# Interleaving the per-head Q/K projections with the attention loop of the head before

## The reference

```python
c_q  = x @ W_DQ                                  # latent 256
Qc   = (c_q @ W_UQ)  -> 16 heads of 64
Qr   = rope(c_q @ W_QR) -> 16 heads of 32
c_kv = x @ W_DKV
Kc   = (c_kv @ W_UK) -> 16 heads of 64
Kr   = rope(x @ W_KR)                            # 32, shared by all heads
V    = (c_kv @ W_UV) -> 16 heads of 64
Q, K = concat([Qc, Qr]), concat([Kc, Kr])        # 96 wide
scores  = clip(Q K^T, -80, 80), causal mask
weights = softmax(scores / sqrt(96))
x = layernorm(x + (weights V) @ W_O)
x = layernorm(x + ffn(x))     # two 8-bit fake-quantised LoRA layers, exact gelu
```

## Time and profile before

| | us |
|---|---|
| median of 3 runs (2410.88 to 2481.31) | 2411.21 |
| the profiled execution | 2413.98 |
| its span on the slowest core (6) | 2412.4 |
| spans of the 8 cores | 2397.9 to 2412.4 |

### The profile page before, as it was taken

How to read it: one execution, slowest core, us unless ns; L and a number is a source line. 1 busy time by engine, 2 the same in 40 slices (tenths; PEclk the granted TensorE clock), 3 DMA queues, 4 the chain that set the end, 5 groups by cost and what they waited for, 6 DMA issues and landing times.

```text
span 2412.4 us, 28275 instructions; the slowest of 8 cores (2397.9 to 2412.4 us)
## 1 busy us (share of the span) xinstructions
PE 1425.3 (59%) x7027; PEld 703.0 (29%) x7038; DVE 1061.8 (44%) x1381; ACT 844.8 (35%) x1165; POOL 83.5 (3%) x136
## 2 busy tenths in 40 slices
PE   0073566666666666564444224331698888988986
PEld 0020122122221222121111002111465655655754
DVE  2257565566665566676445573444212012012012
ACT  0000254444454344450335305555233233233241
POOL 0000000000000000000000000000000000000000
PEclk9576677666677666675665555555798998988987
DMA  5500011111111111412222002323000000000000
GB/s 174 144 6 0 13 51 42 44 55 43 54 43 43 39 60 38 133 38 90 82 75 63 22 10 70 88 87 88 14 19 19 1 19 18 1 19 18 1 18 18
DMA packets 49661, 112.28 MB, mean 47 GB/s; under 512 B 12528, under 2 KB 23280, under 8 KB 47200
## 3 DMA queue, kind: packets, MB, share of 16 engines
q0 software_dynamic: 14912, 54.53, 7.3%
q1 hardware_dynamic: 24800, 34.96, 5.0%
q10 hardware_dynamic: 9792, 20.98, 2.9%
HBM read 97.47 MB, written 8.39 MB: 44 GB/s over the span
## 4 chain that ended last, share of the span: by engine, by line
PE 40%; DVE 24%; ACT 15%; DMA 11%; issue 8%; DVEq 1%; ACTq 1%; SPq 0%; POOLq 0%
PE PSD L314 28%; DVE CL L657 6%; PE PS L314 4%; ACT PT L663 4%; PE BIG L571 4%; DMA QSG<-wPRr 4%; ACT QSG L760 3%; DVE MXW L529 3%; PE PSD L641 3%; DMA QSG<-wFCr 3%; DVE KH L498 2%; DVE CL L650 2%; ACT QH L487 2%; ACT QTI L764 1%; DMA STG<-xT 1%
## 5 line engine op out<-in xcount | busy, mean ns | idle before, releaser
L663 ACT ACTIVATE PT<-CL 128x1024 bf16<-128x1024 f16 (+1 forms) x320 | 310.7, 971 | 363.1 <-DVE CL L650 217.9
L314 PE MATMUL PSD<-XT,RTF 128*128 128x256 bf16 x2048 | 307.9, 300 | 121.7 <-ACT HH L1086 119.8
L641 PE MATMUL PSD<-QH,KH 96*128 96x512 bf16 (+3 forms) x640 | 241.7, 476 | 95.6 <-DVE CL L650 86.9
L571 PE MATMUL BIG<-PT,VP 128*65 128x512 bf16 (+3 forms) x640 | 221.9, 437 | 104.0 <-ACT PT L663 101.6
L314 PE MATMUL PSD<-HH,RTP 128*128 128x256 bf16 x2048 | 237.3, 275 | 53.8 <-DVE UPt L1103 53.8
L657 DVE TENSOR_SCALAR CL<-PSD 128x1024 f16<-128x1024 f32 x192 | 235.2, 1225 | 74.8 <-PE BIG L571 36.5
L314 PEld LDWEIGHTS PSD<-XT,RTF 128*128 128x128 bf16 x2048 | 195.5, 105 | 195.7 <-issue 139.2
L314 PEld LDWEIGHTS PSD<-HH,RTP 128*128 128x128 bf16 x2048 | 196.5, 98 | 85.8 <-issue 55.9
L1086 ACT ACTIVATE HH<-PSD,BFCS,SML 128x256 bf16<-128x256 f32 x256 | 144.3, 564 | 143.5 <-PE PSD L314 130.3
L760 ACT ACTIVATE QSG<-QSG,SML 128x512 f32<-128x512 f32 x128 | 104.0, 813 | 214.6 <-DMA QSG<-wPRr 76.4
L571 PEld LDWEIGHTS BIG<-PT,VP 128*65 128x65 bf16 x640 | 80.7, 127 | 273.4 <-issue 269.1
(11 more groups left out here) (148 smaller groups left out, 1344.3 us busy)
## 6 DMA issues: line engine op xcount, KB each, us to landing
STG<-wFCr POOLq DMA_DIRECT2D x32, 512.0 KB, 4.8
STG<-wPRr POOLq DMA_DIRECT2D x32, 512.0 KB, 4.6
STG<-xT SPq DMA_DIRECT2D x8, 1024.0 KB, 6.2
QSG<-wFCr POOLq DMA_DIRECT2D x32, 256.0 KB, 3.0
QSG<-wFCr ACTq DMA_DIRECT2D x32, 256.0 KB, 2.8
QSG<-wPRr POOLq DMA_DIRECT2D x32, 256.0 KB, 3.3
QSG<-wPRr ACTq DMA_DIRECT2D x32, 256.0 KB, 2.7
out<-OST SPq DMA_DIRECT2D x64, 128.0 KB, 1.9
```

The costliest lines, as they stand in the source:

```text
L314: e.matmul(outap, la, ra, start=st, stop=sp),
L571: qb=qb, kt=kt: e.matmul(self.BIG[0:65, lq:lq + qext], self.VP[:, pcol:pcol + 65], self.PTB[cs][:, off:off + qext], start=(kt == 0), stop= ...
L641: e.matmul(self.PSD[pslot][:, 512 * half: 512 * half + qext], self.KHB[b][0:96, 128 * kt:128 * kt + 128], self.QHB[b][0:96, qlo:qlo + qext ...
L663: etok = P.s(lambda e, cs=cs, qw=qw: e.activation(self.PTB[cs][:, 0:qw], self.CLB[cs][:, 0:qw], AF.Exp, scale=ISQ), waits=[ctok, self.pv_t ...
```

## The change

`emit_production` is split into a list of nine steps: four of Q, the DMA of the rotated rows, four of K. Production 0 is still emitted as a whole ahead of head 0. Production 1 is emitted within head 0, and production h+2 within head h+1: in iterations 1 to 9 of the 20, one step at the end of each iteration, behind its PV matmuls. It still waits for the last scores of head h. So the same instructions are there, in another order. The XFM loads move from behind head 13 to behind head 14.

```diff
     def emit_production(self, h, guard):
+        for step in self.production_steps(h, guard):
+            step()
+
+    def production_steps(self, h, guard):
...
+        return ([q_step(nb) for nb in range(4)] + [qr_step()]
+                + [k_step(nb) for nb in range(4)])
...
         self.emit_production(0, [])
-        self.emit_production(1, [])
+        prod_pending = self.production_steps(1, [])
...
                 while len(pend) > 4:
                     emit_pv(pend.pop(0))
+                if prod_pending and idx >= 2:
+                    prod_pending.pop(0)()
             while pend:
                 emit_pv(pend.pop(0))
+            while prod_pending:
+                prod_pending.pop(0)()
             last_sc[h] = stok
...
             if h + 2 <= 15:
-                self.emit_production(h + 2, [last_sc[h]])
-            if h == 13:
+                prod_pending = self.production_steps(h + 2, [last_sc[h]])
+            if h == 14:
```

More of the change, by code:

```diff
@@ L475, in emit_production @@
     def emit_production(self, h, guard):
+        for step in self.production_steps(h, guard):
+            step()
+    def production_steps(self, h, guard):
         P = self.P
         b = h % 2
[L478 to L509, removed]
+        self.prod[h] = prod = {"kr": self.krk[b]}
+        def q_step(nb):
+            def go():
+                pf = self.prod_free
+                mmtok = self.mmg(
+                    self.PSB[5][0:64, 0:512],
+                    [(self.WUQ[:, D * l + DH * h: D * l + DH * h + DH],
+                      self.CQ[:, 2048 * l + 512 * nb: 2048 * l + 512 * nb + 512])
+                     for l in range(2)],
+                    [self.cq_r, self.wuq_r, pf] + guard)
+                qev = P.s(lambda e, b=b, nb=nb: e.copy(
+                    self.QHB[b][0:64, 512 * nb:512 * nb + 512],
+                    self.PSB[5][0:64, 0:512]), waits=[mmtok] + guard)
+                self.prod_free = qev
+                prod["q"] = qev
+            return go
@@ new lines, in k_step, with go @@
+        def k_step(nb):
+            def go():
+                pf = self.prod_free
+                mmtok = self.mmg(
+                    self.PSB[5][0:64, 0:512],
+                    [(self.WUK[:, D * l + DH * h: D * l + DH * h + DH],
+                      self.CKV[:, 2048 * l + 512 * nb: 2048 * l + 512 * nb + 512])
+                     for l in range(2)],
+                    [self.ckv_r, self.wuk_r, pf] + guard)
+                kev = P.v(lambda e, b=b, nb=nb: e.tensor_copy(
+                    self.KHB[b][0:64, 512 * nb:512 * nb + 512],
+                    self.PSB[5][0:64, 0:512]), waits=[mmtok] + guard)
+                self.prod_free = kev
+                prod["k"] = kev
+            return go
@@ new lines, in qr_step, with go @@
+        def qr_step():
+            def go():
+                prod["qr"] = P.d("sync", "dqr", lambda e, h=h, b=b: e.dma_start(
+                    self.QHB[b][64:96, 0:2048],
+                    self.QRt[32 * (h % 4):32 * (h % 4) + 32,
+                             2048 * (h // 4):2048 * (h // 4) + 2048]),
+                    waits=[self.qr_all, prod["q"], self.x_done_t] + guard)
+            return go
+        return ([q_step(nb) for nb in range(4)] + [qr_step()]
+                + [k_step(nb) for nb in range(4)])
```

## The result

The changed kernel takes 2305.4 us (median of 8 runs, 2302.31 to 2307.89), the kernel before 2411.74 us in the same sessions (8 runs). The ratio is 0.9557, with a 95% interval of 0.9546 to 0.9568: 4.4% less time.

The account below looks back on a forecast made before the run. No attention engine was full; productions between heads ran serially, TensorE and copies waiting on each other over one bank. Removing 203.7 us and adding 97.5 gives 106.2 less: 2305.0 us (chance 0.65), range 2262 to 2343.

Parts of the forecast that it names:

- The production between heads: At 14 head boundaries and ahead of head 0: serial time that goes away, 189 us plus 14.7, 203.7 us in all.
- The reduces are late next: At a head's start: two VectorE reduces, 2.54 us, still precede the first clip; nothing new paid, nothing more gained.
- The Q part: First scores to clip of iteration 6: Q steps wait for copies behind exponentials on ScalarE, adding 3.9 us a head.
- The K part: Clip of iteration 6 to mid-head reduces: four K copies on VectorE make 9.1 us from 6.55, adding 2.6 a head.
- The XFM loads: nothing: ScalarE issues moved one head later: some 4 us lost before, 3.3 after; counted as nothing, -1 to +2 us.
- The second half of a head and phases 3 to 5 stay: After the mid-head reduces and behind the attention stage: second half untouched, phases 3 to 5 as long as before.
- Rival B: First half of a head: added matmuls bring full clock earlier; a head adds 4.0 us, total 2267; chance 0.18.
- C: Second half of a head: clock held at half, 12.2 us a head, total 2390; chance 0.12, shared with other cases.
- D: Iterations with steps: waits for copies close a ring, 22 us a head, total 2537, slower; chance 0.05.
- the walk: One head timed step by step at half clock: Q and K steps add 6.5 us, 97.5 us over 15 heads.

## Why the prediction was right

The forecast was 2305.0 us; measured were 2305.4. That the steps hold is shown below; that the total came within 0.4 us is luck, since the steps are off by up to 4 us each (0.25 us a head in both parts of the loop) and these errors cancel. By its steps:

- *The production between heads is serial time of 13.5 us, 14 times, and 14.7 once.* Right: the gaps fell by 188.4 us in all (189 forecast).
- *The reduces are late next.* Right, shown by moving them: a head is 3.1 us shorter.
- *The Q part costs 3.9 us a head, by the copy behind the exponential.* Right in cause, a little high in size: 3.65 us in the mean (16.6 against 12.95). In head 11 the clip of iteration 6 comes at 768.84 - 751.87 = 17.0 us, where 16.7 was worked out. In heads 4, 6, 9 and 12 it comes at 15.5 to 15.9; there the clock came to full speed some 12 us behind the first scores, in the heads near 17 only after 16.6 us or more. The second bank, and apart from it the doubled distance between steps, took this cost away while the matmuls stayed.
- *The K part costs 2.6 us, by VectorE's copies.* Right in cause, shown by moving them to ScalarE. In heads 3, 8 and 11 the part is 9.8 us, in most heads 9.25, against 9.1 forecast; the mean is 2.8 us above that of before. In all the first halves grew by 6.5 us once the 3.9 us of the XFM issue are taken out of head 14 of before: (388.4 - 290.7) / 15.
- *The XFM loads: nothing.* Right to 1.3 us, a little outside its -1 to +2: 3.9 us went in head 14, 2.65 came in head 15.
- *The second half of a head and phases 3 to 5 stay.* Right: 18.19 us before and after, and +1.7 us behind the stage.

Rival B held in part: the granted clock of the stage rose from 0.69 to 0.77. In heads 4, 6, 9 and 12 the full clock came ahead of the K part, and the clip of iteration 6 came 1.0 to 1.5 us earlier than in the heads near 17. In head 11 it was reached within the K part. The pairs of TensorE's timeline there show it:

```profile
769.27 1.06 PE L314 MATMUL PS<-CKV,WUK 128*64 128x512 bf16 x2
...
774.49 0.59 PE L314 MATMUL PS<-CKV,WUK 128*64 128x512 bf16 x2 [1.29 <-DVE KH L509]
```

There VectorE set the pace, so it brought little: 9.8 us in this head against 9.25 in the heads with the full clock from the start of the K part. The Trainium skill, "TensorE: Matmul & The Clock Gate", section Part 1: The HAM clock gate, says that sustained activity releases the half rate; the trace agrees, since the clock rose here, from 0.69 to 0.77, as the waits of TensorE went. C did not happen: the clock of the second halves rose too, from 0.73 to 0.81 (means of heads 1 to 13). (Its price was worked out low: by its own rows the 17.9 us of matmuls would grow by some 10 us at half clock, not 8.) D did not either: the wait spans two iterations, and costs 4 us a head, not 22.

What the prediction did not see is that the steps' place was so far from the best: the walk priced the wait for Q's copy, but named it as a cost of the change rather than of a distance that one line can double.

## What to carry to other kernels

Work that alternates between two engines over one buffer is cheap inside a loop only if the copy it waits for is older than the loop's own latency: look at what stands ahead of that copy on its engine. Doubling the distance (every second iteration) was worth 60 us and doubling the buffer 50, of which 8 lay ahead of the loop, beside 106 for the move itself. When a serial block goes, look at what each engine does first at the seam; here two reduces that nobody waited for held three engines.

The version that beats both kernels is the one with two banks, K's copies on ScalarE and the reduces within the next head: 0.904 of before, some 230 us less (0.096 x 2411.7), against 106 for the change alone. With the XFM loads on SP's queue it is as fast.

## What the runs showed beside this

Issuing three loads of 1 MB held ScalarE's queue 6.0 to 12.0 us on the slowest cores of these runs though each issue is 0.33 to 0.38 us of busy time; on SP's queue, which it held for 5.95 us, no compute engine waited for it, and the first half of head 15 took 17.4 us in place of 22.0. The granted clock rose as TensorE's waits went: the same matmuls in another order were granted 0.69 and 0.77 of full speed in the attention stage. From the first scores to the clip of iteration 6 it was 0.51 before, 0.64 after and 0.69 with two banks (means of heads 1 to 13). Four gains were larger than their walks (42 us in the heads for 36 with two banks, 36 for 22, 48 for 35, 60 for 34), and the clock is a likely part of it; that was not taken apart.
